# Sliding-window attention and a gated recurrence on one core: softmax division moved from the transposed layout to the values product's own layout

## The chip, the cores and the metric

The kernel runs on one core of a Trainium2 chip. The metric is device microseconds (us) of one execution, the median over runs. An engine is named as in the profile: PE is TensorE's matmul side and PEld its weight loads, DVE is VectorE, ACT is ScalarE, POOL is GpSimd, SP is SyncE, which here only issues DMAs.

## What is computed

Sixteen sequences of 512 tokens and 256 features pass through one block: attention with a window of 128 over 16 heads of 16 features, a residual and layernorm, a gated recurrence whose state runs from sequence to sequence, and a second residual and layernorm. Cut to the parts that matter here:

```python
# attention of one sequence; q, k, v: 16 heads x 512 x 16, blocks of 128 queries see 256 keys
scores = where(valid, q @ k.T / 4 + slope[h] * delta, -inf)
p = softmax(scores, axis=-1)          # exp(s - max) / sum
o = p @ v                             # 16 features per head
x1 = layernorm(x + o @ w_out.T)
# recurrence over the 16 sequences (t), state c: 512 x 256
f, i = sigmoid(x1 @ wf.T + c @ uf.T + bf), sigmoid(x1 @ wi.T + c @ ui.T + bi)
g = tanh(x1 @ wc.T + c @ uc.T + bc)
c = f * c + i * g
# after the last sequence
h = tanh(x1 @ wo.T + c_final @ uo.T + bo)
out = layernorm(x1 + h)
```

The division by the sum is not done on the probabilities. V carries a column of ones beside the 16 features of each head, so the product with the unnormalised probabilities gives, for each head, 16 context rows and one row of sums.

## The kernel before, in words

The program is written by hand for each engine, with semaphores; no scheduler reorders it. `iteration(t)` is written once per engine (lines from about 280, 380, 500, 745 and 1070) and all of them walk through 16 slots, `attend(0)` to `attend(15)`. A slot is one quarter of a group of four heads: on PE the raw scores of sequence t (L940), from which DVE takes the row maxima (L689), and, seven slots later, the scores with the maxima subtracted (L961), which ACT exponentiates (L448) and POOL cuts to the window (L347, L349). Between the slots stands the other work of several sequences: the qkv projections of t+1 and t, the values products and contexts of t-1, the output projection and layernorm of t-2, the gates (L921) and state update of t-3.

Four PSUM banks take everything that is not scores. They are used in two pairs, A0/A1 and B0/B1, which change names from iteration to iteration, so most waits on PE are waits for a bank to be emptied.

**The path of a context.** `values(t, g, bank)` (L975) makes, for group g of four heads, a bank of 128 rows: 32 rows per head, of which 16 are context, one the sum, the rest filler; the columns are the 512 queries. Because each head's sum is a row of that bank, and DVE works along rows, the kernel turns it: ACT copies the bank to `ctx_raw` (`ctx_out`, L459), PE transposes the four 128x128 blocks with the identity (`ctx_transpose`, L983), and DVE, with queries now on the partitions, takes reciprocals of the sum columns (L698) and multiplies (L703) into `o_tok`. This is `normalise`. Per sequence that is 16 transposes in four groups of four, which stand on PE after slots 0, 5, 8 and 13, each behind the values product of the next group. When all four groups are in `o_tok`, PE transposes it back (`o_transpose`, L1016, eight 128x128 blocks after slot 0) so that the features are on the partitions for the output projection, and ACT and DVE split it into a high and a low part (`ot_hi` L465, `ot_lo`, L661).

`ctx_raw` is a single buffer. `ctx_out` of a group waits until PE has transposed the group before it:

```python
wait(act, pv_ready, 4, t, g + 1)
wait(act, ct_ready, 4, t, g)
sc.activation(ctx_raw[:, :], bank[:, :], ACT.Copy).then_inc(ctx_done, 1)
```

On PE the gates of slot 1 write into bank A1, from which `ctx_out(t-1, 1)` reads, and so wait for it: `wait(pe, ctx_done, 4, t - 1, 2)`.

**The DMA queue.** SP issues nearly all DMAs in one order. Its busiest duty is to write q and k of each projection to DRAM (`parts_to_dram`, L239, two bursts of four DMAs of 256 KB per sequence) and read them back in the stacked layout that the scores need (`stack`, L254, four times eight DMAs). Each group's row maxima also go by DMA into the stack (`max_to_stack`, L262). SP is in order: what waits there holds everything written behind it.

After the 16 iterations `last_sequences` finishes the open sequences, and a last stage computes `h` and the second layernorm for all sequences. Wo and Uo, the weights of that stage, are loaded and split into high and low parts at the start.

## Time and profile before

| | |
|---|---|
| median of 3 runs | 1004.26 us (1003.01 to 1005.67) |
| the profiled execution, its own time | 1004.63 us |
| its span, first to last instruction | 1002.9 us |
| PE busy | 915.2 us, 91% |
| PEld busy | 753.2 us, 75% |
| DVE busy | 719.0 us, 72% |
| ACT busy | 575.9 us, 57% |
| POOL busy | 407.6 us, 41% |
| mean granted TensorE clock | 0.953 of full |
| moved by DMA | 131.86 MB |

The time of an execution is its span and 1.7 us around it. Busy shares are means over start, sixteen iterations, and end, each with its own limit; the iterations make up most of the span, and what limits one of them is read from its timeline.

### The profile page before, as it was taken

The page shows a single profiled execution, that of the slowest core. Times are in us where ns is not written, and L with a number is a line of the kernel's source. Part 1 is how long each engine was busy: PE and PEld are TensorE (multiplying, and loading weights), DVE is VectorE, ACT ScalarE, POOL GpSimd, SP SyncE. Part 2 cuts the span into 40 slices and gives each one's busy share as a digit, 9 for nine tenths or more (in the row PEclk, how much of TensorE's full clock was granted, in tenths as well). Part 3 has the DMA queues.
Part 4 walks back from the last instruction along what each step waited for, and adds up shares of the span by engine and source line. Part 5 has one row for each costly group of instructions (what it writes and reads, how often), then busy time and mean ns, then how long its engine had stood idle before and what let it go on. Part 6 is the DMA issues. An engine that isn't in the chain of part 4 may idle for free.

```text
span 1002.9 us, 25924 instructions
## 1 busy us (share of the span) xinstructions
PE 915.2 (91%) x9500; PEld 753.2 (75%) x9500; DVE 719.0 (72%) x2795; ACT 575.9 (57%) x1167; POOL 407.6 (41%) x687
## 2 busy tenths in 40 slices
PE   3587879999999999999999999999999989889994
PEld 2375668878788878788878787878787867668884
DVE  7766576877777777777777778787878673327885
ACT  5144556555656565656565656565756464325886
POOL 5142443354444444444444444444444353101443
PEclk9577889999999999999999999999999999899998
DMA  7634443535454545444544454444444400121764
GB/s 257 168 117 121 129 140 126 151 120 143 135 140 137 138 138 139 139 137 139 134 143 133 144 129 146 129 147 129 146 108 145 124 28 22 42 91 49 221 202 132
DMA packets 93534, 131.86 MB, mean 131 GB/s; under 512 B 12128, under 2 KB 47584, under 8 KB 93408
## 3 DMA queue, kind: packets, MB, share of 16 engines
q1 hardware_dynamic: 93136, 129.95, 44.2%
q8 instruction: 76, 1.25, 0.5%
q14 instruction: 50, 0.41, 0.1%
q10 hardware_dynamic: 272, 0.26, 0.1%
HBM read 79.31 MB, written 50.33 MB: 129 GB/s over the span
## 4 chain that ended last, share of the span: by engine, by line
PE 64%; DVE 25%; ACT 5%; issue 4%; POOL 2%; DMA 0%; ACTq 0%; DVEq 0%; POOLq 0%
PE bank L921 29%; DVE bank L689 11%; PE bank L909 11%; PE bank L940 8%; PE bank L975 7%; PE bank L961 3%; DVE max_q L689 3%; DVE qk_parts L661 2%; PE bank L983 2%; DVE gate L738 2%; DVE gate L736 1%; PE bank L1016 1%; PE bank L1029 1%; ACT Pt L643 1%; DVE stats L877 1%
## 5 line engine op out<-in xcount | busy, mean ns | idle before, releaser
L689 DVE CUSTOM_DVE_ANT_0 bank<-bank,mask 128x256 f32<-128x256 f32 (+1 forms) x1024 | 369.3, 423 | 136.1 <-PE bank L940 134.5
L448 ACT ACTIVATE Pt<-bank 128x512 f32<-128x512 f32 (+1 forms) x512 | 248.2, 536 | 204.1 <-PE bank L961 204.0
L347 POOL TENSOR_SCALAR_AFFINE_SELECT Pt<-Pt 128x512 f32<-128x512 f32 x256 | 174.7, 682 | 414.8 <-ACT Pt L448 414.8
L940 PE MATMUL bank<-Ks,Qs 59*128 59x256 f32 (+1 forms) x1024 | 149.5, 320 | 51.3 <-DVE max_q L689 40.5
L940 PEld LDWEIGHTS bank<-Ks,Qs 59*128 59x128 f32 x1024 | 108.5, 192 | 94.8 <-DVE max_q L689 54.5
L689 DVE DVE_READ_ACCUMULATOR2_ANT max_q<- 128x1 f32 x1024 | 144.6, 141 | 0.0
L349 POOL TENSOR_SCALAR_AFFINE_SELECT Pt<-Pt 128x384 f32<-128x384 f32 x256 | 139.3, 544 | 0.0
L975 PE MATMUL bank<-Pt,Vp 128*32 128x256 f32 (+1 forms) x2048 | 131.2, 377 | 0.0
L921 PE MATMUL bank<-x1T,Wg 64*128 64x512 f32 x960 | 128.0, 398 | 0.8 <-DVE o_tok L703 0.8
L921 PE MATMUL bank<-cT,Ug 64*128 64x512 f32 x960 | 125.8, 393 | 0.0
L961 PE MATMUL bank<-Qs,Ks 60*128 60x256 f32 (+1 forms) x1024 | 112.1, 271 | 0.4 <-ACT Pt L448 0.3
L975 PEld LDWEIGHTS bank<-Pt,Vp 128*32 128x32 f32 x2048 | 81.5, 116 | 32.1 <-issue 8.2
L921 PEld LDWEIGHTS bank<-cT,Ug 64*128 64x128 f32 x960 | 89.6, 184 | 17.7
L921 PEld LDWEIGHTS bank<-x1T,Wg 64*128 64x128 f32 x960 | 87.4, 185 | 18.6 <-DVE o_tok L703 0.9
L961 PEld LDWEIGHTS bank<-Qs,Ks 60*128 60x128 f32 x1024 | 95.7, 193 | 2.3 <-issue 1.3
L486 ACT ACTIVATE gate<-bank,bias_half 128x512 f32<-128x512 f32 x64 | 42.5, 687 | 44.7 <-PE bank L921 23.9
L459 ACT ACTIVATE ctx_raw<-bank 128x512 f32<-128x512 f32 x64 | 38.2, 597 | 49.7 <-PE bank L983 47.6
L909 PE MATMUL bank<-xT,Win 128*128 128x512 f32 x204 | 55.5, 425 | 8.6 <-DVE Win L661 8.6
L921 PE MATMUL bank<-Win,xT 64*128 64x256 f32 x768 | 56.7, 291 | 0.0
L909 PEld LDWEIGHTS bank<-xT,Win 128*128 128x128 f32 x204 | 40.5, 205 | 17.6 <-DVE Win L661 8.6
L921 PEld LDWEIGHTS bank<-Win,xT 64*128 64x128 f32 x768 | 52.8, 197 | 0.0
L661 DVE SCALAR_TENSOR_TENSOR qk_parts<-bank,qk_parts 128x512 fp32r<-128x512 f32 x64 | 42.6, 686 | 14.2 <-ACT qk_parts L431 14.2
(111 smaller groups left out, 1345.7 us busy)
## 6 DMA issues: line engine op xcount, KB each, us to landing
parts_dram<-qk_parts SPq DMA_DIRECT2D x128, 256.0 KB
Qs<-parts_dram SPq DMA_DIRECT2D x128, 128.0 KB, 2.6
Ks<-parts_dram SPq DMA_DIRECT2D x128, 128.0 KB, 2.7
xt_raw<-in_xt SPq DMA_DIRECT2D x16, 512.0 KB, 4.2
Qs<-parts_dram SPq DMA_DIRECT2D x128, 64.0 KB, 2.6
Ks<-parts_dram SPq DMA_DIRECT2D x128, 64.0 KB, 2.7
x_res<-in_x SPq DMA_DIRECT2D x16, 512.0 KB, 3.9
x_dram<-y SPq DMA_DIRECT2D x16, 512.0 KB, 3.7
```

What stands on the lines that cost most here:

```text
L347: gp.affine_select(out=p4[:, :, 0:128], in_=p4[:, :, 0:128], compare_op=ALU.is_ge, fill=0.0, base=0, pattern=[[0, 4], [1, 128]], channel_m ...
L349: gp.affine_select(out=p4[:, 0:3, 128:256], in_=p4[:, 0:3, 128:256], compare_op=ALU.is_ge, fill=0.0, base=0, pattern=[[0, 3], [-1, 128]], ...
L448: sc.activation(probabilities(g, 2 * pair + odd)[:, S * a:S * a + n], SC[odd][:, 0:n], ACT.Exp).then_inc(exp_done, 1)
L459: sc.activation(ctx_raw[:, :], bank[:, :], ACT.Copy).then_inc(ctx_done, 1)
L486: ins = sc.activation(gate[:, k if k == 3 else which, :], bank[:, :], ACT.Tanh, bias=bias_half[:, which, j:j + 1], scale=0.5)
L661: return ve.scalar_tensor_tensor(out_, in_, scale, hi.bitcast(F32), op0=ALU.mult, op1=ALU.subtract)
L689: ins = ve.tensor_tensor_reduce(out=raw, in0=raw, in1=mask[:, keys], scale=1.0, scalar=MASKED, op0=ALU.add, op1=ALU.max, accum_out=max_q[: ...
L909: ins = te.matmul(out_, w, m, start=(first and n == 0), stop=(last and n == len(todo) - 1))
L921: ins = te.matmul(out_, w(r), m(r), start=(turn == 0 and opens and n == 0), stop=final, skip_group_check=True)
L940: ins = te.matmul(MX[odd][:, 256 * (n % 2):256 * (n % 2) + 256][:, keys], Qs[rows, 2 * g + pair, n * WIN:(n + 1) * WIN], Ks[rows, 2 * g + ...
L961: ins = te.matmul(SC[odd][:, 256 * (j % 2):256 * (j % 2) + width], Ks[rows, 2 * g + pair, j * WIN:(j + 1) * WIN], Qs[rows, 2 * g + pair, j ...
L975: ins = te.matmul(bank[32 * hh:32 * hh + 32, j * WIN:j * WIN + width], Vp[:, j, PITCH * h:PITCH * h + 32], probabilities(g, hh)[:, 256 * j ...
```

## The change

The contexts stay in the layout in which the values product makes them. `ctx_transpose`, `o_transpose` and `normalise` go for sequences 0 to 14; for the last sequence they stay, under names that begin with `last_`. In their place:

- `store_ctx(t, g)`: SP writes `ctx_raw` to DRAM after each `ctx_out`; and `ctx_out` of a group now waits for the landing of the store of the group before it.
- `load_denominators`: SP waits for the four stores and gathers the 16 rows of sums, 512 queries each, as four blocks of 16 x 128 into `den_q`. DVE turns them (32x32 block transposes of a 128x128 tile), inverts them and turns them back; SP writes the result to DRAM (`store_inverses`) and, once that has landed, reads it back with each row repeated for the 16 features of its head (`spread_inverses`), twice 128x512.
- `load_contexts`: SP reads the context rows alone, packed, into `o_un`, twice 128x512.
- POOL multiplies the two (`scale_contexts`, twice 128x512, at the head of an iteration), and ACT and DVE split the product from SBUF into `oT` (`ot_hi` is moved behind slot 1, `ot_lo` behind slot 2).

Wo and Uo now share the place of Win and are loaded and split during the last sequences (ACT three activations, POOL two subtractions). The state update is cut in two: its first product (`forget`) is done earlier than the rest (`take_in`), after slots 0 and 6.

```diff
+            def store_ctx(t, g):
+
+                wait(sp, ctx_done, 4, t, g + 1)
+                sp.dma_start(ctx_dram[t % 2, g], ctx_raw[:, :]).then_inc(ctx_stored[g], 16)
+
+            def load_denominators(t):
+
+                sp.wait_ge(den_cleared, 1)
+                for g in range(QUADS):
+                    wait(sp, ctx_stored[g], 16, t, 16)
+                wait(sp, inv_stored, 16, t - 1, 16)
+                rows = ctx_dram[t % 2].rearrange("g (h r) (q i) -> q (g h) r i", r=2 * D, i=128)[:, :, D, :]
+                for q in range(4):
+                    sp.dma_start(den_q[32 * q:32 * q + H, :], rows[q]).then_inc(den_in, 16)
+
+            def load_contexts(t, c):
+                wait(sp, otlo_done, 2, t - 1, c + 1)
+                rows = ctx_dram[t % 2, 2 * c:2 * c + 2].rearrange("g (h r) s -> (g h) r s", r=2 * D)[:, 0:D, :]
+                sp.dma_start(o_un[:, c, :], rows).then_inc(o_un_in[c], 16)
+
+            def store_inverses(t):
+                wait(sp, inv_turned, 1, t, 1)
+                sp.dma_start(inv_dram[t % 2].rearrange("r (q i) -> q r i", i=128), den_q[:, :]).then_inc(inv_stored, 16)
+
+            def spread_inverses(t):
+
+                wait(sp, inv_stored, 16, t, 16)
+                for c in range(KC):
+                    wait(sp, scaled_done, 2, t - 1, c + 1)
+                    rows = inv_dram[t % 2, 8 * c:8 * c + 8]
+                    sp.dma_start(inv_den[:, c, :], rows.unsqueeze(1).to_broadcast([8, D, S])).then_inc(inv_in[c], 16)
+
...
                 p1, p2, n1, now = real(t - 1), real(t - 2), real(t + 1), real(t)
+                by_rows = p1 and t - 1 < B - 1
                 if p1: max_to_stack(t - 1, 3)
                 if now: stack(t, 1)
                 if p2:
                     wait(sp, y_done, 2, t - 3, 2)
                     sp.dma_start(x_res[:, :, :], x[t - 2].rearrange(tok, p=128)).then_inc(xres_in, 16)
+                if by_rows: store_ctx(t - 1, 1)
                 if real(t + 2): load_xt(t + 2)
                 if now:
                     stack(t, 2)
                     max_to_stack(t, 0)
-                    stack(t, 3)
+                if by_rows: store_ctx(t - 1, 2)
+                if now: stack(t, 3)
                 if n1: parts_to_dram(t + 1, 0)
                 if now: max_to_stack(t, 1)
+                if by_rows: store_ctx(t - 1, 3)
                 if p2:
                     wait(sp, x1_done, 4, t - 2, 4)
                     sp.dma_start(x1_dram[t - 2].rearrange(tok, p=128), y[:, :, :]).then_inc(x1_out, 16)
+                if by_rows:
+                    load_denominators(t - 1)
+                    for c in range(KC):
+                        load_contexts(t - 1, c)
                 if n1: stack(t + 1, 0)
                 if now: max_to_stack(t, 2)
-                if n1: parts_to_dram(t + 1, 1)
+                if by_rows:
+                    store_inverses(t - 1)
+                    spread_inverses(t - 1)
+                if n1:
+                    parts_to_dram(t + 1, 1)
+                    store_ctx(t, 0)
+                if t == B - 1: load_last_weights()
...
+            def scale_contexts(t, c):
+
+                wait(pool, o_un_in[c], 16, t, 16)
+                wait(pool, inv_in[c], 16, t, 16)
+                gp.tensor_tensor(o_un[:, c, :], o_un[:, c, :], inv_den[:, c, :], ALU.mult).then_inc(scaled_done, 1)
+
...
+                        scale_contexts(t - 2, c)
                 if p1:
                     for hh in range(4):
...
             def ctx_out(t, g, bank):
                 wait(act, pv_ready, 4, t, g + 1)
-                wait(act, ct_ready, 4, t, g)
+                pt, pg = before(t, g)
+                if pt < B - 1:
+                    wait(act, ctx_stored[pg], 16, pt, 16)
+                else:
+                    act.wait_ge(ct_ready, g)
                 sc.activation(ctx_raw[:, :], bank[:, :], ACT.Copy).then_inc(ctx_done, 1)
 
-            def ot_hi(t, c, bank):
+            def ot_hi(t, c):
                 if c == 0:
                     wait(act, op_ready, 2, t - 1, 2)
-                wait(act, ot_ready, 2, t, c + 1)
+                wait(act, scaled_done, 2, t, c + 1)
+                sc.activation(oT[:, 0, c, :], o_un[:, c, :], ACT.Copy).then_inc(othi_done, 1)
...
@@ -508,11 +607,11 @@
                 if p1: max_row(t - 1, 3, A0)
                 attend(0)
                 if p1: ctx_out(t - 1, 1, A1)
-                if p2:
-                    ot_hi(t - 2, 0, B0)
-                    ot_hi(t - 2, 1, B1)
                 attend(1)
                 if n1: x_hi(t + 1, 0)
+                if p2:
+                    ot_hi(t - 2, 0)
+                    ot_hi(t - 2, 1)
...
+            def turn_denominators(t):
+
+                wait(dve, den_in, 64, t, 64)
+                ve.transpose(den_t[:, :], den_q[:, :]).then_inc(den_turned, 1)
+
+            def invert_denominators(t):
+                wait(dve, den_turned, 1, t, 1)
+                own = den_t[:, :].rearrange("p (b r) -> p b r", r=32)[:, :, 0:H]
+                ve.reciprocal(own, own).then_inc(den_inverted, 1)
+
+            def turn_inverses(t):
+                wait(dve, den_inverted, 1, t, 1)
+                ve.transpose(den_q[:, :], den_t[:, :]).then_inc(inv_turned, 1)
+
+            def ot_lo(t, c):
+                wait(dve, othi_done, 2, t, c + 1)
+                minus_hi(oT[:, 1, c, :], o_un[:, c, :], oT[:, 0, c, :]).then_inc(otlo_done, 1)
+
...
+            def forget(t, j):
+
+                wait(dve, gate_done, 6, t, 3 * j + 1)
+                wait(dve, c_done, 2, t - 1, j + 1)
+                ve.scalar_tensor_tensor(gate[:, 3 * j, :], gate[:, 3 * j, :], 1.0, c2[:, j, :], op0=ALU.add, op1=ALU.mult).then_inc(kept_done, 1)
+
+            def take_in(t, j):
+                wait(dve, gate_done, 6, t, 3 * j + 3)
+                ve.scalar_tensor_tensor(gate[:, 1, :], gate[:, 1, :], 1.0, gate[:, 2, :], op0=ALU.add, op1=ALU.mult).then_inc(taken_done, 1)
+                wait(dve, kept_done, 2, t, j + 1)
+                wait(dve, taken_done, 2, t, j + 1)
+                wait(dve, chi_done, 2, t - 1, j + 1)
...
@@ -751,14 +878,14 @@
                     maxima(t, slot // 4, slot % 4)
 
                 attend(0)
-                if p1: normalise(t - 1, 0, A0)
-                if p2:
-                    ot_lo(t - 2, 0, B0)
-                    ot_lo(t - 2, 1, B1)
+                if p3: forget(t - 3, 0)
                 attend(1)
                 if n1: x_lo(t + 1, 0)
                 attend(2)
                 if n1: x_lo(t + 1, 1)
+                if p2:
+                    ot_lo(t - 2, 0)
...
                 attend(7)
-                if p3: update(t - 3, 0)
+                if p3: take_in(t - 3, 0)
                 attend(8)
-                if p3: update(t - 3, 1)
-                if p1: normalise(t - 1, 2, B0)
+                if p3: take_in(t - 3, 1)
                 attend(9)
                 attend(10)
                 attend(11)
                 attend(12)
                 if n1: qk_lo(t + 1, 2, B0)
                 attend(13)
+                if p1: turn_denominators(t - 1)
                 if n1: qk_lo(t + 1, 3, B1)
-                if p1: normalise(t - 1, 3, A0)
-                if p2:
-                    x1_lo(t - 2, 0, B0)
-                    x1_lo(t - 2, 1, B1)
+                if p1: invert_denominators(t - 1)
+                if p2: x1_lo(t - 2, 0, B0)
+                if p1: turn_inverses(t - 1)
+                if p2: x1_lo(t - 2, 1, B1)
...
-                    wait(pe, gate_done, 6, t - 3, 1)
-                    o_transpose(t - 2, 0, B0)
-                    freed(pe, (gate_done, 6, t - 3, 2), (ctx_done, 4, t - 1, 1))
-                    o_transpose(t - 2, 1, B1)
 
                 attend(1)
                 if p3:
                     g2, g3 = gate_halves(2, A0), gate_halves(3, A1)
-                    wait(pe, o_done, 4, t - 1, 1)
+                    wait(pe, maxrow_done, 4, t - 1, 4)
                     wait(pe, ctx_done, 4, t - 1, 2)
                     abreast(g2, g3, 0, None)
                 attend(2)
@@ -1094,19 +1214,19 @@
                 attend(3)
                 if p2:
                     o0, o1 = out_halves(0, B0), out_halves(1, B1)
+                    freed(pe, (gate_done, 6, t - 3, 1), (maxrow_done, 4, t - 1, 3))
+                    freed(pe, (gate_done, 6, t - 3, 2), (ctx_done, 4, t - 1, 1))
                     wait(pe, otlo_done, 2, t - 2, 2)
                     abreast(o0, o1, 0, None)
                 attend(4)
                 if p2: abreast(o0, o1, 1, op_ready)
 
                 attend(5)
-                freed(pe, (gate_done, 6, t - 3, 3), (o_done, 4, t - 1, 1), (qklo_done, 4, t, 3))
+                freed(pe, (gate_done, 6, t - 3, 3), (maxrow_done, 4, t - 1, 4), (qklo_done, 4, t, 3))
```

Two places of the order show what moves. The first is the end of an iteration on SP, before; `max_rows` are the row maxima of groups 2 and, behind the burst, 3, and `parts_dram` is where q and k go:

```order
L262 DMA Qs<-max_rows 1x8x128 [waits maxrow_done]
L262 DMA Qs<-max_rows 1x8x128
L239 DMA parts_dram<-qk_parts 8x16x512 [waits qklo_done,stacked3,stacked2]
L239 DMA parts_dram<-qk_parts 8x16x512
L239 DMA parts_dram<-qk_parts 8x16x512 [waits qklo_done]
L239 DMA parts_dram<-qk_parts 8x16x512
L262 DMA Qs<-max_rows 1x8x128 [waits maxrow_done]
L262 DMA Qs<-max_rows 1x8x128
L254 DMA Qs<-parts_dram 32x2x512 [waits q_parts_out0,sc_ready]
```

The same place after the change, where `ctx_raw` going to `ctx_dram` is `store_ctx(t, 0)`:

```order
L275 DMA Qs<-max_rows 1x8x128 [waits maxrow_done]
L275 DMA Qs<-max_rows 1x8x128
L300 DMA inv_dram<-den_q 4x32x128 [waits inv_turned]
L308 DMA inv_den<-inv_dram 128x1x512 [waits scaled_done,inv_stored]
L308 DMA inv_den<-inv_dram 128x1x512 [waits scaled_done]
L252 DMA parts_dram<-qk_parts 8x16x512 [waits qklo_done,stacked3,stacked2]
L252 DMA parts_dram<-qk_parts 8x16x512
L252 DMA parts_dram<-qk_parts 8x16x512 [waits qklo_done]
L252 DMA parts_dram<-qk_parts 8x16x512
L281 DMA ctx_dram<-ctx_raw 128x512 [waits ctx_done]
L275 DMA Qs<-max_rows 1x8x128 [waits maxrow_done]
L275 DMA Qs<-max_rows 1x8x128
```

Between the maxima of group 2 and the burst stand three DMAs with two waits, on DVE's second turn and on the landing of the inverses; the store of the context stands behind the burst and ahead of the maxima of group 3.

The second is PE from the end of slot 0's values product to the gates of slot 1, before:

```order
L975 MATMUL bank<-Pt,Vp 32x128 x4
L983 MATMUL bank<-ident,ctx_raw 128x128 [waits ctx_done,maxrow_done]
L983 MATMUL bank<-ident,ctx_raw 128x128 x3
L1016 MATMUL bank<-ident,o_tok 128x128 [waits o_done,gate_done]
L1016 MATMUL bank<-ident,o_tok 128x128 x3
L1016 MATMUL bank<-ident,o_tok 128x128 [waits o_done,gate_done]
L1016 MATMUL bank<-ident,o_tok 128x128 x3
L940 MATMUL bank<-Ks,Qs 128x256 [waits red_done] x2
L940 MATMUL bank<-Ks,Qs 128x256 x2
L961 MATMUL bank<-Qs,Ks 128x256 [waits exp_done] x2
L961 MATMUL bank<-Qs,Ks 128x256 x2
L921 MATMUL bank<-x1T,Wg 128x512 [waits ctx_done,o_done]
L921 MATMUL bank<-x1T,Wg 128x512 x11
```

and after:

```order
L1102 MATMUL bank<-Pt,Vp 32x256 [waits masked_done,x1lo_done]
L1102 MATMUL bank<-Pt,Vp 32x256 x11
L1102 MATMUL bank<-Pt,Vp 32x128 x4
L1067 MATMUL bank<-Ks,Qs 128x256 [waits red_done] x2
L1067 MATMUL bank<-Ks,Qs 128x256 x2
L1088 MATMUL bank<-Qs,Ks 128x256 [waits exp_done] x2
L1088 MATMUL bank<-Qs,Ks 128x256 x2
L1048 MATMUL bank<-x1T,Wg 128x512 [waits ctx_done,maxrow_done]
L1048 MATMUL bank<-x1T,Wg 128x512 x11
```

The twelve transposes are gone, and the gates, whose wait for `ctx_done` is the one for ACT's copy of group 1, come directly behind the scores of slot 1.

## Rows read from the trace of the kernel before

**Rows 1.** The page, busy time of each engine: us, share, instructions
```profile
PE 915.2 (91%) x9500; PEld 753.2 (75%) x9500; DVE 719.0 (72%) x2795; ACT 575.9 (57%) x1167; POOL 407.6 (41%) x687
```

**Rows 2.** Windows, 50 us of the middle: busy us (instructions) per engine, clock, DMA share
```profile
466.00:516.00 50.00, 48.97 (x571) 40.65 (x566) 38.65 (x162) 30.90 (x64) 22.22 (x38) 1.00 0.49 139
```

**Rows 3.** Timeline of PE, one iteration: start, us, what [idle before it]
```profile
480.17 1.66 PE L921 MATMUL bank<-x1T,Wg 64*128 64x512 f32 x12
...
492.93 0.66 PE L983 MATMUL bank<-ident,ctx_raw 128*128 128x128 f32 x4
493.34 3.02 PE L909 MATMUL bank<-xT,Win 128*128 128x512 f32 x12
...
505.29 0.66 PE L983 MATMUL bank<-ident,ctx_raw 128*128 128x128 f32 x4
505.87 0.51 PE L940 MATMUL bank<-Ks,Qs 59*128 59x256 f32 x4
...
508.54 0.32 PE L940 MATMUL bank<-Ks,Qs 59*128 59x128 f32 x1 [0.49 <-DVE max_q L689]
509.30 0.49 PE L940 MATMUL bank<-Ks,Qs 59*128 59x128 f32 x3 [0.44 <-DVE max_q L689]
...
518.28 1.35 PE L1029 MATMUL bank<-ident,y 128*128 128x128 f32 x8
...
528.53 0.66 PE L983 MATMUL bank<-ident,ctx_raw 128*128 128x128 f32 x4
...
529.99 0.51 PE L940 MATMUL bank<-Ks,Qs 59*128 59x256 f32 x4
...
530.64 1.67 PE L921 MATMUL bank<-x1T,Wg 64*128 64x512 f32 x12
```

**Rows 4.** Timeline of DVE, same iteration
```profile
518.23 0.69 DVE L661 SCALAR_TENSOR_TENSOR qk_parts<-bank,qk_parts 128x512 fp32r<-128x512 f32 x1
...
519.65 1.34 DVE L661 SCALAR_TENSOR_TENSOR x1T<-bank,x1T 128x512 fp32r<-128x512 f32 x2
```

**Rows 5.** Groups by line: busy us, mean ns of one, idle before
```profile
L364 POOL TENSOR_TENSOR cT<-c,cT 128x512 fp32r<-128x512 f32 x26 | 32.7, 1275 | 0.0
```

**Rows 6.** The page, DMA issues: KB each, median us to landing
```profile
Qs<-parts_dram SPq DMA_DIRECT2D x128, 64.0 KB, 2.6
...
x_dram<-y SPq DMA_DIRECT2D x16, 512.0 KB, 3.7
```

**Rows 7.** The tile parts_dram: landings min/median/max
```profile
DMA to landing us min/median/max: 2.0/2.7/5.1
```

**Rows 8.** Timeline of SP, same iteration: the time is that of issuing
```profile
483.75 0.43 SPq L275 DMA_DIRECT2D x_res<-in_x  x1
...
516.73 1.41 SPq L262 DMA_DIRECT2D Qs<-max_rows  x2
518.57 3.27 SPq L239 DMA_DIRECT2D parts_dram<-qk_parts  x4
```

**Rows 9.** Windows of 1 us behind that burst
```profile
521.00:522.00 1.00, 1.00 (x12) 0.78 (x12) 1.00 (x7) 0.15 (x1) 1.00 (x3) 1.00 0.51 190
525.00:526.00 1.00, 1.00 (x12) 0.79 (x10) 0.00 (x0) 0.00 (x0) 0.00 (x0) 1.00 0.52 199
526.00:527.00 1.00, 1.00 (x21) 0.88 (x21) 0.27 (x3) 0.55 (x1) 0.00 (x0) 1.00 0.19 68
```

**Rows 10.** Timeline of ACT, same iteration
```profile
529.28 0.60 ACT L459 ACTIVATE ctx_raw<-bank 128x512 f32<-128x512 f32 x1 [0.69 <-PE bank L983]
```

**Rows 11.** Windows near the end, behind a pause of PE
```profile
857.00:861.00 4.00, 3.75 (x28) 2.53 (x32) 1.38 (x2) 1.30 (x3) 0.00 (x0) 0.50 0.66 197
861.00:865.00 4.00, 4.00 (x36) 2.93 (x29) 0.00 (x0) 0.60 (x1) 0.00 (x0) 0.98 0.20 70
```

**Rows 12.** Timeline of PE near the end
```profile
857.25 1.94 PE L1029 MATMUL bank<-ident,y 128*128 128x128 f32 x8 [3.99 <-ACT y L470]
```

**Rows 13.** Timeline of DVE at the start
```profile
24.78 5.57 DVE L661 SCALAR_TENSOR_TENSOR cT<-c,cT 128x512 fp32r<-128x512 f32 x2 [1.16 <-ACT cT L613]
```

More of the change, by code:

```diff
@@ L299, in _ @@
             sp.wait_ge(xt_ready, 2 * B)
+            sp.wait_ge(last_lo, 2)
             def load(t, i):
@@ L606, in _ @@
                 qk_hi(0, k, banks[4 + (k + 2) % 4])
-            act.wait_ge(weights_in, 80)
-            for n in range(5):
+            act.wait_ge(weights_in, 48)
+            for n in range(3):
                 weights_hi(n)
```

172 lines of the change are left out of this document (96 added, 76 removed).

## The prediction

> **What bounds the kernel now.** I read the page first. PE is busy for 91% of the span [rows 1], and a stretch of 50 us in the middle, one iteration, says it more sharply: PE 48.97 of 50 us at full clock, DVE 38.65, ACT 30.90, POOL 22.22 [rows 2]. So in the iterations PE's own order of work sets the time, and everything else counts only where PE waits for it. The timeline of PE then shows what the change can take from it and where it waits: one iteration lasts 50.5 us (the gates of slot 1 begin at 480.17 and again at 530.64), and inside it PE waits only twice, 0.49 and 0.44 us, for DVE's maxima behind the state update and a `normalise` [rows 3]. All times below are on the clock of this iteration; sequence numbers are those of the code.
>
> **What goes.** Per iteration PE loses 16 context and 8 output transposes. I price them by start to next start, since they are pipelined: after slot 0, 528.53 to 529.99 = 1.46 us; after slot 5, 492.93 to 493.34 = 0.41; after slot 8, 505.29 to 505.87 = 0.58 [rows 3]. The fourth group, after slot 13, I price at nothing: the x1 transposes behind it need DVE's low part of k, which ends at 518.9, while the first of them starts at 518.28 [rows 3, 4]. Take the context transposes away, and PE arrives earlier and waits for DVE, which now also turns the sums there. The two waits of 0.93 us go too: `normalise` and the first product of the update are no longer in front of slot 9's maxima. Together 1.46 + 0.41 + 0.58 + 0.93 = 3.38 us per iteration. DVE and ACT lose and gain small instructions; with 11 and 19 us idle per iteration that costs nothing as long as they are not waited for. POOL gains two multiplications, 1.28 us each by its nearest row [rows 5], beside some 28 idle us; the windows behind them are of the group whose values product comes only after slot 5.
>
> **What is added, and what it waits for.** The price lies in one wait. `ctx_out(t, 1)` now needs the landing of `store_ctx(t, 0)`, and on SP that store stands at the very end of the iteration: behind `store_inverses`, behind its landing, behind two spreads and behind a burst of four stores of q and k. PE's gates of slot 1 wait for this `ctx_out`. I follow that chain.
>
> 1. DVE. The inverses are turned back behind the first low part of x1. The pair of those started at 519.65 and took 1.34 [rows 4], so the first ends at about 520.3. I take 520.4; SP has by then issued its row maxima (516.73 plus what is new ahead of it, about 1 us), so DVE comes last.
> 2. `store_inverses`, 64 KB, must land before SP goes on. No row shows this shape. The nearest is a 64 KB load of 2.6 us [rows 6]; it is cut into pieces of 2 KB, this one into four times as many of 512 B. The longest landing seen on this path is 5.1 [rows 7]. I take 3.3, near the first: 523.7.
> 3. Two spreads. An issue costs 0.43 us for a plain tile and 3.27 / 4 = 0.82 for the 8x16x512 pattern of the parts [rows 8]; these have that pattern on the DRAM side, so 1.6 together. The burst begins at 525.3 (at 0.43 each, 524.6).
> 4. The burst. The one issued from 518.57 keeps the DMA engines at a share of 0.51 to 0.52 and 190 to 199 GB/s from 521 on, and in the slice from 526 little is left (0.19) [rows 8, 9]. Its data end at 526.3, 7.7 us after the first issue: half the engines carry 1 MB, and issuing it faster would not help. The spreads' 512 KB have the same row count of 8; at 190 GB/s they take 2.75 us. The first data of a burst came 2.1 us after its issue, so theirs run from 525.8 to 528.5, and the burst's own first data (525.3 + 2.1 = 527.4) are pushed back by 1.15. End of the burst: 525.3 + 7.7 + 1.15 = 534.15.
> 5. `store_ctx(t, 0)`, 256 KB over all engines. Half of it lies on the engines that still carry the burst: 128 KB at 190 GB/s is 0.7, and 0.5 for the semaphore by my estimate: 535.35. If its share did not queue there, it would land 3.7 us at most after its own issue, the median of a store of 512 KB [rows 6]: 525.3 + 3.3 + 3.7 = 532.3.
> 6. ACT copies the bank, 0.60 [rows 10]: 535.95. PE's gates start at 536.0. Unforced they would have started at 530.64 - 1.46 = 529.2. PE waits 6.8 us.
>
> Step 5 is where a rule decides. The rows show only that half of the engines are busy while the parts go out, and with my reading that a later store waits for them the wait is 6.8. The Trainium skill says so too ("DMA: Bandwidth & Descriptors", HWDGE ordering): each engine consumes its descriptors in ring order. By that rule the store lands at 535.35 and the execution takes 1077; with a store that overtakes the burst the wait is 3.8 and the sum gives 1035. The same page (how many engines) makes the inverses' store, whose outer count is 4, run on 4 engines only; no row here shows such a store.
>
> **The clock.** When PE stood idle for 3.99 us near the end, the granted clock was 0.50 (1.2 GHz, of 2.4) for the 4 us after it went on, and 0.98 in the 4 us behind them [rows 11, 12]. Half the speed for 4 us costs 2.0. A wait of 6.8 us should do the same in each iteration.
>
> **The sum.** Per full iteration: - 3.38 + 6.8 + 2.0 = + 5.4; for t = 3 to 15, thirteen of them, + 70.5. Iteration 2 has the wait, but I count no clock loss, since its clock is unsteady already: + 3.4. Iteration 1 is bound by DVE, which loses four `normalise`: - 2. At the start DVE needed 5.57 us for two low parts of the state, whose like takes 0.68 later, beside POOL splitting the weights [rows 4, 13]; with Wo and Uo gone I take - 2. In the last sequences three activations come in front of the layernorm for which PE already waits [rows 12], 3 x 0.60 = + 1.8, the output transposes of sequence 14 go, - 1.0, and its contexts arrive late, + 1.5. Sum: 70.5 + 3.4 - 2 - 2 + 2.3 = + 72.2. The profiled execution took 1004.63 with a span of 1002.9; 1004.63 + 72.2 = 1076.8. The median of the runs is 0.4 below that execution, which changes nothing: **1077 us**.
>
> **Bounds.** With every step of the chain at its cheapest (2.6, two issues of 0.43, no push, but the burst in front: 523.0 + 0.86 + 7.7 + 0.7 + 0.5 = 532.75, gates at 533.4) PE waits 4.2 and an iteration costs + 2.8: 36.7 + 0.8 for iteration 2 - 1.7 for the rest is + 36, or 1040. With the dearest (a landing of 5.1, and two issues of 0.82) it waits 8.6: + 7.2, or 93.9 + 5.2 - 1.7 = + 97, 1102.
>
> **The rivals.**
> - *The store is in time, and the change is faster.* The place is the same: it decides whether `store_ctx(t, 0)` lands before 528.6, when the values product of the next group is done. Then 13 x 3.38 = 43.9, 3.4 in iteration 2 and 1.7 for the rest go: 956. For it speaks that PE is full and that what is taken away is PE's; against it, that even the cheapest chain with no queueing (523.0 + 0.86 + four issues of 0.82 + 3.7) gives 530.9. In between, with such a landing and a wait of 2.3 us, too short to cost much clock, an iteration still gains 1.1: 988. I give 0.08 to the first and 0.09 to the second.
> - *The wait is there, but short or without the clock.* The store does not queue, or PE's pause doesn't cost the clock: 6.8 without the clock is + 3.4 per iteration, 1051; 3.8 with the clock is + 2.4, 1035; 3.8 without it is + 0.4, 1009. What lies below 1040 has 0.15.
> - *The split of oT becomes the wait.* `ot_lo` now stands behind slot 2's maxima and is wanted in slot 3; if the store were in time, PE would wait there for some 0.5 us: 13 x 0.5 = 6.5 back, 962. It speaks for itself in the order, but behind a wait of 6.8 us in slot 1 it is hidden. It is in the chance of the first rival.
> - *DVE waits for the sums.* `turn_denominators` stands in DVE's row before slot 14. The fourth context lands at about 510, the gathers at 514, and DVE arrives at 518.4: 4 us to spare. Were it late, every us would be one of PE's: 0.04, above 1102.
>
> **How the numbers follow.** The main case, 1040 to 1102, has 0.64. A measurement of this kernel can tell 0.3%, 3 us, from no change. Slower by more: 0.64 + 0.04 + nearly all of the 0.15, so 0.81; same, 0.03; faster, 0.16. The range must leave out no more than 2 in 10: it takes in the main case and what lies below it down to 1005, where only the faster cases remain, and ends at 1102.
>
> **What would show it.** In the profile of the changed kernel, ACT's `ctx_raw` copy of group 1 should start about 7 us after the values product of slot 0 has ended, released by the DMA that stores group 0; PE's gates of slot 1 should show that idle time, and an iteration should last about 56 us with a granted clock near 0.95 and not 1.00. SP should wait for DVE's second turn and then for the landing of the inverses. The prediction is wrong if PE's longest wait per iteration is elsewhere, if the store lands less than 8 us after the first issue of the burst before it, or if the iterations are shorter than 50.5 us.

## The result and the profile after

The changed kernel takes **1137.06 us** (median of 4 runs, 1134.24 to 1141.48) against 1004.35 (1003.01 to 1005.67): a ratio of 1.1325, 95% interval 1.1286 to 1.1365. The forecast was 1077 and the range 1005 to 1102: the direction was right, the size missed by 60 us.

From the page of the changed kernel, busy time of the engines and the groups with the largest waits (columns as in [rows 5]):

```profile
PE 912.4 (80%) x9140; PEld 747.0 (66%) x9140; DVE 714.2 (63%) x2721; ACT 574.0 (50%) x1167; POOL 452.1 (40%) x717
...
L1048 PE MATMUL bank<-x1T,Wg 64*128 64x512 f32 x960 | 147.9, 445 | 91.1 <-ACT ctx_raw L543 91.1
...
L543 ACT ACTIVATE ctx_raw<-bank 128x512 f32<-128x512 f32 x64 | 37.9, 592 | 115.8 <-DMA ctx_dram<-ctx_raw 100.5
```

PE was busy for 91% [rows 1] and is now for 80%. The forecast wait is there: the gates wait 91.1 us for ACT's context copy, and the copy for the DMA. The waits of PE show what else there is (us in total, times, longest us):

```profile
PE bank L1048 <- ACT ctx_raw L543: 91.1, 14, 8.7
PE bank L1067 <- DVE max_q L789: 28.6, 52, 1.5
PE bank L1088 <- DMA Qs<-max_rows: 26.0, 19, 3.6
...
PE bank L1048 <- DVE oT L761: 14.1, 13, 2.0
```

L1088 is the second scores product, which waits for the row maxima on their way through SP's queue. No step of the forecast has that wait, and the one for oT was to be hidden. One iteration on SP shows the forecast chain. The first number of a row is the start of its first issue, the second the time that issuing took, and not the landing:

```profile
587.73 1.78 SPq L291 DMA_DIRECT2D den_q<-ctx_dram  x4
589.56 1.45 SPq L296 DMA_DIRECT2D o_un<-ctx_dram  x2
591.13 1.80 SPq L267 DMA_DIRECT2D Qs<-parts_dram  x4
592.97 1.82 SPq L267 DMA_DIRECT2D Ks<-parts_dram  x4
594.84 1.36 SPq L275 DMA_DIRECT2D Qs<-max_rows  x2
596.24 0.56 SPq L300 DMA_DIRECT2D inv_dram<-den_q  x1
601.24 1.27 SPq L308 DMA_DIRECT2D inv_den<-inv_dram  x2
602.62 4.01 SPq L252 DMA_DIRECT2D parts_dram<-qk_parts  x4
606.67 1.44 SPq L281 DMA_DIRECT2D ctx_dram<-ctx_raw  x1
608.16 2.74 SPq L275 DMA_DIRECT2D Qs<-max_rows  x2
```

and on PE, where the two waits stand 14 us apart; the last row is ACT's copy, which releases the second:

```profile
601.21 0.51 PE L1088 MATMUL bank<-Qs,Ks 60*128 60x256 f32 x4 [2.21 <-DMA Qs<-max_rows]
601.55 2.25 PE L1048 MATMUL bank<-cT,Ug 64*128 64x512 f32 x12
...
615.00 2.93 PE L1048 MATMUL bank<-x1T,Wg 64*128 64x512 f32 x12 [6.02 <-ACT ctx_raw L543]
```
```profile
614.25 0.60 ACT L543 ACTIVATE ctx_raw<-bank 128x512 f32<-128x512 f32 x1 [5.95 <-DMA ctx_dram<-ctx_raw]
```

The granted clock of the same stretch, in windows of 1 us (length, PE busy, clock, DMA share, GB/s); the windows left out in 604 and from 613 to 618 are all at 0.50:

```profile
601.00:602.00 1.00, 0.79 (x8) 1.00 0.00 0
602.00:603.00 1.00, 1.00 (x8) 0.59 0.15 55
603.00:604.00 1.00, 1.00 (x6) 0.50 0.46 174
...
605.00:606.00 1.00, 1.00 (x12) 0.71 0.48 152
606.00:607.00 1.00, 1.00 (x23) 1.00 0.49 176
...
612.00:613.00 1.00, 0.00 (x0) 0.71 0.78 256
...
618.00:619.00 1.00, 1.00 (x7) 0.50 1.09 402
619.00:620.00 1.00, 1.00 (x12) 0.88 0.27 94
620.00:621.00 1.00, 1.00 (x16) 1.00 0.00 0
```

About 1 us after PE has gone on behind the pause of 2.2 us, the clock falls to half (1.2 GHz) and stays there from about 602.2 to 605.6. PE, busy all the while, loses half of these 3.4 us, 1.7. In the pause of 6.0 us the clock falls at 612.4 and stays low until 619.2; 4.2 us of that are behind the pause, 2.1 us lost.

**An account of one iteration**, made the same way for every kernel below: from its PE timeline the period (x1 transposes to x1 transposes, mean of twelve iterations of the middle), the idle time before PE's instructions by releaser, and the rest. At full clock the rest is PE's own work, 46.4 to 46.5 us in the two kernels without the DMA path (x4, x8); what lies above that in the other kernels with the change is mostly the clock (the kernel before has its transposes there). Taken from the granted clock instead, as half of the time that PE was busy at half clock, the loss is 3.2 us an iteration in the changed kernel, 2.5 in x2, 0.7 in x11 and 0.1 in x7.

The columns between are waits: for ACT's context copy, for the row maxima, for Ks (the keys that `stack` reads back) and for oT (DVE's low part), each by the instruction that needs it; "x1 transposes" is what they wait for the low part of k, "DVE's maxima" what the raw scores wait for.

| kernel, us per iteration | period | wait for ctx_raw | row maxima | Ks | oT | x1 transposes | DVE's maxima | other | rest |
|---|---|---|---|---|---|---|---|---|---|
| before | 50.49 | 0 | 0 | 0 | 0 | 0 | 1.10 | 0.1 | 49.33 |
| changed | 60.38 | 7.00 | 1.66 | 0 | 0.93 | 0.71 | 0.60 | 0 | 49.48 |
| x1_early_store | 52.26 | 0.18 | 2.19 | 0.45 | 0.72 | 0.72 | 0.62 | 0 | 47.38 |
| x2_contexts_late | 58.68 | 7.70 | 0.23 | 0 | 0.92 | 0.69 | 0.62 | 0 | 48.51 |
| x3_both | 49.79 | 0.18 | 0.46 | 0.55 | 0.51 | 0.69 | 0.62 | 0 | 46.77 |
| x4_no_dma | 49.06 | 0.18 | 0.24 | 0 | 0.90 | 0.69 | 0.62 | 0 | 46.42 |
| x5_before_burst | 52.92 | 0.83 | 2.37 | 0 | 0.84 | 0.70 | 0.60 | 0 | 47.58 |
| x6_burst_first | 53.78 | 0.18 | 0.13 | 0 | 0 | 0.53 | 0.77 | 3.9 | 48.29 |
| x7_dve_order | 50.23 | 0.17 | 0.74 | 1.42 | 0 | 0.52 | 0.62 | 0 | 46.76 |
| x8_no_dma_order | 48.37 | 0.18 | 0.16 | 0 | 0 | 0.52 | 0.97 | 0 | 46.54 |
| x9_middle | 57.28 | 4.19 | 1.78 | 0 | 0.93 | 0.71 | 0.59 | 0 | 49.09 |
| x10_pool_queue | 53.64 | 0.18 | 0.23 | 0 | 0 | 0.52 | 0.82 | 3.2 | 48.70 |
| x11_sooner | 50.00 | 0.16 | 0.44 | 0.79 | 0 | 0.81 | 0.74 | 0 | 47.05 |

The "other" of x6 and x10 is a wait of the scores product for ACT's probabilities. Three numbers of the changed kernel's row (row maxima 1.66, oT and x1 transposes 1.64 together, and a rest 3.0 above 46.5) are the matter of the experiments.

### The profile page after: what moved, and what is told of

It reads as the page before. It is cut to its first block and busy times, and to the rows that moved or that the text cites. A ratio compares the mean times of both kernels' runs of the same rounds, so it can differ in the third digit from the quotient of the medians.

```text
span 1139.7 us, 25314 instructions
## 1 busy us (share of the span) xinstructions
PE 912.4 (80%) x9140; PEld 747.0 (66%) x9140; DVE 714.2 (63%) x2721; ACT 574.0 (50%) x1167; POOL 452.1 (40%) x717
## 5 line engine op out<-in xcount | busy, mean ns | idle before, releaser
L1048 PE MATMUL bank<-x1T,Wg 64*128 64x512 f32 x960 | 147.9, 445 | 91.1 <-ACT ctx_raw L543 91.1
L1067 PE MATMUL bank<-Ks,Qs 59*128 59x256 f32 (+1 forms) x1024 | 146.2, 323 | 44.9 <-DVE max_q L789 28.6
L1048 PEld LDWEIGHTS bank<-x1T,Wg 64*128 64x128 f32 x960 | 103.4, 213 | 110.8 <-issue 93.5
L415 POOL TENSOR_SCALAR_AFFINE_SELECT Pt<-Pt 128x384 f32<-128x384 f32 x256 | 146.2, 571 | 0.0
L1088 PE MATMUL bank<-Qs,Ks 60*128 60x256 f32 (+1 forms) x1024 | 114.5, 279 | 31.0 <-DMA Qs<-max_rows 26.0
L1048 PE MATMUL bank<-cT,Ug 64*128 64x512 f32 x960 | 139.2, 425 | 0.0
L1088 PEld LDWEIGHTS bank<-Qs,Ks 60*128 60x128 f32 x1024 | 95.6, 198 | 38.0 <-DMA Qs<-max_rows 30.2
L1048 PEld LDWEIGHTS bank<-cT,Ug 64*128 64x128 f32 x960 | 102.5, 206 | 18.5
L761 DVE SCALAR_TENSOR_TENSOR xT<-xt_raw,xT 128x512 fp32r<-128x512 f32 x32 | 23.3, 732 | 97.5 <-ACT xT L506 97.5
L436 POOL TENSOR_TENSOR o_un<-o_un,inv_den 128x512 f32<-128x512 f32 x30 | 39.0, 1301 | 96.7 <-DMA inv_den<-inv_dram 96.7
L1048 PE MATMUL bank<-Wout,oT 64*128 64x256 f32 x672 | 48.5, 287 | 14.1 <-DVE oT L761 14.1
```

The costliest lines, as they stand in the source:

```text
L415: gp.affine_select(out=p4[:, 0:3, 128:256], in_=p4[:, 0:3, 128:256], compare_op=ALU.is_ge, fill=0.0, base=0, pattern=[[0, 3], [-1, 128]], ...
L436: gp.tensor_tensor(o_un[:, c, :], o_un[:, c, :], inv_den[:, c, :], ALU.mult).then_inc(scaled_done, 1)
L1048: ins = te.matmul(out_, w(r), m(r), start=(turn == 0 and opens and n == 0), stop=final, skip_group_check=True)
L1067: ins = te.matmul(MX[odd][:, 256 * (n % 2):256 * (n % 2) + 256][:, keys], Qs[rows, 2 * g + pair, n * WIN:(n + 1) * WIN], Ks[rows, 2 * g + ...
L1088: ins = te.matmul(SC[odd][:, 256 * (j % 2):256 * (j % 2) + width], Ks[rows, 2 * g + pair, j * WIN:(j + 1) * WIN], Qs[rows, 2 * g + pair, j ...
```

## The experiments

Line numbers shift by one or two between the kernels; the operations are the same. SP's order of one iteration, as changed: the gather of the sums, the contexts' loads, `stack(t+1, 0)`, `max_to_stack(t, 2)`, the inverses' store, its landing, the spreads, the burst, `store_ctx(t, 0)`.

**x1_early_store** takes the store out from behind everything:

```diff
                 if now: max_to_stack(t, 2)
+                if n1: store_ctx(t, 0)
                 if by_rows:
                     store_inverses(t - 1)
...
                     parts_to_dram(t + 1, 1)
-                    store_ctx(t, 0)
```

> The change with store_ctx(t, 0) moved ahead of the inverses' store and the burst, directly behind the row maxima of group 2. Theory A (the place of this store on SP makes PE's wait in slot 1): the wait of PE's gates for ACT's ctx_raw copy, 7.0 us per iteration as a mean of twelve, goes with some 2.5 us of lost clock; the waits for the row maxima (about 2) and for oT (1.0) stay. An iteration falls from 60.4 to about 51, the kernel to about 1012 us. Theory B (the DMA engines are overloaded as a whole, wherever the store stands): the wait comes back at another landing, and the kernel stays above 1080.

Measured 1030.6 us (1024.71 to 1034.87), ratio 1.0257 (1.0217 to 1.0297), 19 us above the expected 1012. The wait for the context copy is gone, and 106 us with it, but the row maxima stayed and grew:

```profile
PE bank L1087 <- DMA Qs<-max_rows: 33.0, 21, 3.2
PE bank L1066 <- DVE max_q L788: 28.9, 53, 1.5
PE bank L1066 <- DMA Ks<-parts_dram: 21.9, 11, 11.5
PE bank L1047 <- DVE oT L760: 9.7, 10, 1.0
```

So the place of the store is the main cause, and not the only one.

**x2_contexts_late** asks where the maxima's wait comes from. The contexts' loads are the DMAs issued ahead of the stack and the maxima, and nobody needs them before the inverses:

```diff
                     load_denominators(t - 1)
-                    for c in range(KC):
-                        load_contexts(t - 1, c)
...
                     store_inverses(t - 1)
+                    for c in range(KC):
+                        load_contexts(t - 1, c)
                     spread_inverses(t - 1)
```

> The change with load_contexts (two loads of 256 KB with an outer count of 8) moved from ahead of the stack and the row maxima of group 2 to behind the inverses' store. If the maxima land late because these loads lie ahead of them on the engines, PE's wait for them (about 2 us in slot 15) goes. Theory A then says that the chain to the context's store still ends at the same distance from slot 13, so the wait in slot 1 grows by as much: 1125 to 1140. If the two waits are independent, some 35 us go: about 1100.

Measured 1113.68 us (1111.43 to 1117.89), ratio 1.1093. The maxima's wait fell from 1.66 to 0.23 us. And the landing of the inverses' store, for which SP stood still, fell too. SP's wait in the changed kernel, and here:

```profile
SPq L308 <- DMA inv_dram<-den_q: 55.6, 15, 4.8
```
```profile
SPq L308 <- DMA inv_dram<-den_q: 7.9, 15, 0.6
```

So it was not the store's shape: 512 KB of contexts' loads, with the stack behind them, had stood in its way. The spreads now start 2.5 us after the inverses' store, and not 5.0. Yet the context store gained nothing from it:

```profile
587.24 0.56 SPq L300 DMA_DIRECT2D inv_dram<-den_q  x1
587.84 1.25 SPq L296 DMA_DIRECT2D o_un<-ctx_dram  x2
589.71 1.19 SPq L308 DMA_DIRECT2D inv_den<-inv_dram  x2
591.01 2.47 SPq L252 DMA_DIRECT2D parts_dram<-qk_parts  x4
593.53 0.60 SPq L281 DMA_DIRECT2D ctx_dram<-ctx_raw  x1
```
```profile
602.76 0.60 ACT L543 ACTIVATE ctx_raw<-bank 128x512 f32<-128x512 f32 x1 [8.44 <-DMA ctx_dram<-ctx_raw]
```

The store is issued quickly, at 593.53, and it is 9.2 us from there to ACT's copy, which waits for its landing: the data of 2 MB issued in the 6 us before it are in front of it. So the wait did grow (7.00 to 7.70 us), by less than half of what the maxima gave back; with the second pause some clock loss went too (rest 49.48 to 48.51), and an iteration is 1.7 us shorter.

**x3_both** has both moves, with the context's store ahead of the inverses' store and the contexts' loads behind it.

> Both moves. Theory A: both waits go; an iteration is 47.1 (50.5 - 3.4) plus the 1.0 us wait for oT and perhaps 0.5 at the x1 transposes, 48.5 us: about 980 us, faster than before the change (1004). Theory B: above 1050.

Measured 998.33 us (996.93 to 1000.6), ratio 0.9947 (0.9929 to 0.9966): 139 us less than the changed kernel, and below the kernel before. With these two moves the change is a gain of half a per cent; 18 us of the expected gain are missing.

**x4_no_dma** says whether the DMA path keeps them. It drops `store_ctx` 1 to 3 and 0, the gathers, the loads, the inverses' store and the spreads, and fills `o_un`, `inv_den` and `den_q` with ones, so the attention output of sequences 0 to 14 is left out; POOL's, DVE's and ACT's instructions stay.

```diff
-                if by_rows: store_ctx(t - 1, 1)
...
-                wait(dve, den_in, 64, t, 64)
...
-                wait(pool, o_un_in[c], 16, t, 16)
-                wait(pool, inv_in[c], 16, t, 16)
+                wait(pool, otlo_done, 2, t - 1, c + 1)
```

> The change without its DMA path: no context, sum or inverse is stored or loaded for sequences 0 to 14, and ACT doesn't wait for a store; POOL multiplies tiles of ones, DVE turns and inverts a tile of ones, so that the attention output of these sequences is left out. It prices what the change takes off PE, with no new DMA. My sum gives - 3.38 us per iteration and 956 us. If it comes out near 1004, the transposes were worth nothing to begin with.

Measured 984.0 us (983.15 to 986.29), ratio 0.9801 (0.9784 to 0.9817). So even a free path would not give the forecast's 956. PE's work did shrink, by 49.33 - 46.42 = 2.9 us an iteration; but the waits behind it grew:

```profile
PE bank L1033 <- DVE oT L747: 13.8, 13, 2.0
PE bank L1141 <- DVE qk_parts L747: 8.9, 13, 0.8
```

**x5_before_burst** splits the chain of the context store. It puts the store behind the inverses' landing and the spreads, as changed, but ahead of the burst.

```diff
                 if n1:
-                    parts_to_dram(t + 1, 1)
                     store_ctx(t, 0)
+                    parts_to_dram(t + 1, 1)
```

> The only edit to the changed kernel: store_ctx(t, 0) moves from behind the burst of four stores of q and k to directly ahead of it, still behind the store of the inverses, its landing and the two spreads. Theory A (the burst in front of it on the queue and on half the DMA engines is what delays the store; the inverses' chain alone would do no harm): the store is issued near the place where the first store of the burst stood, lands some 4 us later, before the values product of slot 0 has ended, and PE's wait for the context copy (7.0 us an iteration) goes, with its clock loss: 1030 to 1040 us, as with the store ahead of the whole chain (1030.6). Rival B (the landing of the inverses and the spreads' 512 KB are enough by themselves to make it late): a wait of 2 to 4 us stays with its clock loss of some 2 us, 1070 to 1095 us.

Measured 1035.56 us (1029.48 to 1039.06), ratio 1.0307 (1.0272 to 1.0342): theory A. The inverses' landing still costs SP 56.7 us, and PE hardly waits for ctx_raw (0.83).

**x9_middle** puts the store between the two stores of q and the two of k.

```diff
                 for which in range(2):
+                    if which and between is not None: store_ctx(between, 0)
...
-                    parts_to_dram(t + 1, 1)
-                    store_ctx(t, 0)
+                    parts_to_dram(t + 1, 1, t)
```

> The only edit to the changed kernel: store_ctx(t, 0) goes into the middle of the burst, behind its two stores of q and ahead of its two of k. Behind the whole burst PE waited 7.0 us an iteration for it (1137.1 us), ahead of the burst hardly at all (1035.6). Theory A (the store's data queue behind whatever was issued before it): half a burst in front is 512 KB on half of the engines, 3.9 us of data less than a whole one, so PE waits some 3 us an iteration and the time is 1080 to 1095 us, clock loss included. Rival B (only the time of its own issue counts, 2 us earlier than behind the burst, and the data don't queue): a wait of 5 us stays, 1105 to 1120 us.

Measured 1101.59 us (1096.58 to 1103.11), ratio 1.0965: between the two theories, with a wait of 4.2 where they had 3 and 5. From the start of the store's issue to ACT's copy in one iteration of each, when ACT stood waiting for it: 5.2 us with only the spreads in front (599.95 to 605.17 in x5), 6.6 with half a burst (586.17 to 592.72), 7.6 with a whole one (606.67 to 614.25), and 9.2 in x2. The median landing of all context stores in x3 is 3.5. So both act: the store leaves SP later, and its data are held up by what is in front. The Trainium skill ("DMA: Bandwidth & Descriptors", HWDGE ordering) says that each DMA engine consumes its descriptors in ring order, and this growth is in accord with it; a store that overtook what is in front would have kept one landing time in all of them. That the transfers in flight merely share the engines' time would lengthen the landing too, and these runs don't tell the two apart.

**x7_dve_order** is x3 with two moves on DVE.

```diff
-                if n1: x_lo(t + 1, 1)
                 if p2:
                     ot_lo(t - 2, 0)
                     ot_lo(t - 2, 1)
+                if n1: x_lo(t + 1, 1)
...
-                if p1: turn_denominators(t - 1)
                 if n1: qk_lo(t + 1, 3, B1)
+                if p1: turn_denominators(t - 1)
```

> The kernel with both moves on SP's queue (998.3 us), and two moves on DVE: ot_lo(0) and ot_lo(1) ahead of x_lo(t + 1, 1) instead of behind it, and turn_denominators behind qk_lo(t + 1, 3) instead of ahead of it. Theory: PE's wait of 0.4 to 1.0 us for oT in slot 3 and some 0.25 of the 0.75 us before the x1 transposes go, so about 0.9 us in each of 13 iterations: 986 us. Rival: what PE saves there it spends waiting for the row maxima and for Ks of the stack, since the DMA's times don't move: 995 to 998 us.

Measured 1002.55 us (996.75 to 1006.32, 12 runs), ratio 0.9982 (0.9963 to 1.0001): the rival, and 4.6 us above its range. The wait for oT went (0.51 to 0), and Ks and the row maxima took it over (1.01 to 2.16 together).

**x8_no_dma_order** makes the same two moves where no DMA can take over (x4).

> The kernel without the DMA path of the contexts (984.0 us; tiles of ones stand in for the loaded contexts and inverses, so the attention output of sequences 0 to 14 is left out), with the same two moves on DVE as in x7_dve_order. It asks why that kernel gained 20 us and not the forecast 48. Theory A: 1.0 us an iteration is the wait for oT and 0.3 us the turn of the sums ahead of the low part of k, 13 x 1.3 = 17 us: 967 us. Rival B: PE's order has other dependences on DVE and ACT that take over, and it stays at 980 to 984 us.

Measured 975.79 us (973.39 to 977.05), ratio 0.9715 (0.9697 to 0.9734). The 0.9 for oT went; of the wait at the x1 transposes only 0.17, since they then wait for the low part of k itself, and DVE's maxima took 0.35. With the clock full and no DMA in the way, 2.8 us less work for PE (49.33 - 46.54) shortened the iteration by 2.1.

**x6_burst_first** and **x10_pool_queue** try to start the burst sooner, on x7. The first moves it ahead of the inverses' store and the contexts' loads:

```diff
+                if n1: parts_to_dram(t + 1, 1)
                 if by_rows:
                     store_inverses(t - 1)
...
                     spread_inverses(t - 1)
-                if n1: parts_to_dram(t + 1, 1)
```

> The kernel of x7_dve_order with one more move on SP: the burst parts_to_dram(t + 1, 1) goes ahead of the inverses' store, the contexts' loads and the spreads. Theory A: the burst starts some 3 us earlier, so Ks and the row maxima behind it land earlier and PE's waits for them (0.4 to 1.1 us each) go; the spreads land late, but before ot_lo is wanted: 975 to 982 us. Rival B: the inverses' chain behind a burst of 1 MB lands 6 us or more later, oT is late for slot 3, and PE waits there 2 to 4 us with a clock loss: 1010 to 1050 us.

> The kernel of x7_dve_order with the inverses' store and the two spreads issued by POOL instead of SP (store ahead of the last four windows of the iteration, spreads behind them), so that SP doesn't wait for their landing and the burst is issued some 4 us earlier. Theory A: Ks and the row maxima behind the burst land earlier, their waits (some 2 us an iteration) go, and the inverses, on a queue of their own, are not held up: 975 to 985 us. Rival B: the DMA engines are shared all the same, the inverses and spreads land late behind the burst's data, oT is late and PE waits at slot 2 or 3, as with the burst first (1055 us): 1010 us or more.

x6 measured 1055.08 us (1047.41 to 1062.31), x10 1041.65 (1038.02 to 1047.05), ratios 1.0507 (1.0472 to 1.0543) and 1.0371 (1.0349 to 1.0392): rival B both times, x6 even 5 us above its range. Ks is in time, but the inverses and the spreads are behind the burst. In x10, whose inverses have a queue of their own, POOL's rows of one iteration read:

```profile
602.40 1.22 POOL L427 DMA_DIRECT2D inv_den<-inv_dram  x2 [0.40 <-DMA inv_dram<-den_q]
610.58 1.29 POOL L433 TENSOR_TENSOR o_un<-o_un,inv_den 128x512 f32<-128x512 f32 x1 [6.96 <-DMA inv_den<-inv_dram]
613.47 1.26 POOL L433 TENSOR_TENSOR o_un<-o_un,inv_den 128x512 f32<-128x512 f32 x1 [1.60 <-DMA inv_den<-inv_dram]
```

8.2 us from the spreads' issue to the first product, where x3 has 6.05 (569.98 to 576.03). ACT waits for the products at `ot_hi`, and with it, in order, the probabilities that PE wants: 3.9 and 3.2 us an iteration. So a queue of their own did not help: the spreads still landed late behind the burst's data, which SP had issued from 598.20 on. That the shared DMA engines hold them up is the reading that fits; no run separates it from another cause on POOL's queue.

**x11_sooner** leaves the order of the queue and starts the inverses earlier, on x7:

```diff
                 attend(12)
+                if p1:
+                    turn_denominators(t - 1)
+                    invert_denominators(t - 1)
+                    turn_inverses(t - 1)
                 if n1: qk_lo(t + 1, 2, B0)
...
-                if p1: turn_denominators(t - 1)
-                if p1: invert_denominators(t - 1)
...
-                if p1: turn_inverses(t - 1)
...
+                if by_rows: store_inverses(t - 1)
                 if now: max_to_stack(t, 2)
                 if n1: store_ctx(t, 0)
                 if by_rows:
-                    store_inverses(t - 1)
```

> The kernel of x7_dve_order with the sums turned, inverted and turned back in a row directly behind slot 12's maxima, in DVE's gap of 0.9 us before qk_lo(t + 1, 2), some 3 us sooner than now, and the inverses' store ahead of max_to_stack(t, 2) on SP. Theory A (PE's remaining waits for Ks and the row maxima, 2.2 us an iteration, come from the burst starting late behind the spreads): the inverses are stored 2 us sooner, the spreads and the burst start 1 to 1.5 us sooner, and 1 to 1.5 us of those waits go: 983 to 990 us. Rival B: the fourth gather of the sums lands only about when DVE gets there, DVE waits for it, and PE waits for the low part of k and the x1 transposes in turn: 1000 to 1015 us.

Measured 995.9 us (990.57 to 1000.38), ratio 0.9922 (0.9893 to 0.9952): short of theory A, and 0.8% below the kernel before. Its median is the lowest of the complete versions here, but its interval overlaps that of x3 (0.9929 to 0.9966), so the two are not told apart. Against x7, Ks and the row maxima together fell from 2.16 to 1.23 us an iteration, while the x1 transposes (+ 0.29), DVE's maxima (+ 0.12) and the rest (+ 0.29) gave most of that back. The rest is the clock: in the twelve iterations of x11 it was at half five times, from 333.7, 364.4, 408.8, 756.9 and 808.1, for 3.4 us each, the first four behind pauses of PE of 1.4 to 2.1 us. In x7 that happened once.

## Why the prediction was right and wrong

**The wait in slot 1** was forecast in its place and size: 6.8 us against 7.0. The size is right by luck. In the iteration shown, from the inverses' issue (step 1) to ACT's copy (step 6), the forecast has 535.35 - 520.4 = 14.95 us, the trace 614.25 - 596.24 = 18.0:

- step 2, the landing of `store_inverses`: 3.3 forecast, 5.0 measured. The step failed by taking the price from the size of the transfer and not from what is issued ahead of it. With the contexts' loads out of the way the spreads start 2.5 us behind it (x2).
- step 3, two spreads: 1.6, measured 1.38.
- steps 4 and 5, burst and store: 10.05, measured 11.63 (602.62 to 614.25). Right in kind (x5, x9); the issues alone grew to 4.01 + 1.44, from 3.27 [rows 8] and 0.43.

The chain was 3.05 us longer, but PE reached the place 3.9 later as well, by the 2.2 us of its other wait and 1.7 of clock: 6.8 + 3.05 - 3.9 = 5.95, and the row shows 6.02.

**The sum per iteration** was + 5.4; it is + 9.9 (60.38 - 50.49). The step that failed is the one that let a single wait carry the price: the row maxima's way through the same queue was counted as nothing once SP had issued them, and it costs 1.66 us of waiting and 0.7 to 1.0 us of clock an iteration. Term by term against the account:

| term | forecast | measured |
|---|---|---|
| transposes gone | - 2.45 | - 2.9 (49.33 - 46.42, x4) |
| DVE's waits gone | - 0.93 | - 0.57 (with o_tok) |
| wait for ctx_raw | + 6.8 | + 7.0 |
| wait for the row maxima | not in the sum | + 1.66 |
| oT, "hidden" | 0 | + 0.93 |
| x1 transposes | 0 | + 0.71 |
| clock | + 2.0 | + 3.0 |

1. *Missing: the row maxima.* This is the largest flaw of the working. "SP has by then issued its row maxima" was said of the issue alone. They are issued at 594.84 and PE goes on at 601.21, 6.4 us later, because they stand behind contexts' loads and a stack. x2 shows it by 1.43 us of wait less with one move.
2. *oT.* "Behind a wait of 6.8 us in slot 1 it is hidden" is wrong: the wait passes through ACT, and `ot_hi` stands behind `ctx_out` there, so oT is late by as much as PE is. 0.93 us stay with the wait of slot 1 and 0.90 without it (x4); the move on DVE takes them away (x7, x8). The forecast had 0.5.
3. *Slot 13 "at nothing"* holds as a net price: PE's work fell by 0.4 more than the three other groups make, and 0.71 of waiting came for it.
4. *The clock.* 2.0 us for one long pause is what a kernel with one such pause shows: x2, rest 48.51 against 46.5. The changed kernel has 3.0. In five of the twelve iterations the clock is at half for another 3.4 us behind a wait of 1.9 to 2.4 us for the row maxima, 1.7 us lost each time, or 0.7 an iteration of the 1.0. So the term was about right for the long pause, and there was one too few, which goes back to point 1. The rivals took "a wait of 2.3 us" to be "too short to cost much clock"; here one of 2.2 us cost 1.7.

The differences are - 0.4 + 0.4 + 0.2 + 1.7 + 0.9 + 0.7 + 1.0 = 4.5 us an iteration, or 58 us for 13. The span grew by 136.8 us (1139.7 - 1002.9), 64.6 more than the forecast 72.2; the profiled execution is the longest of the four. Of the 6.6 that remain, the start has most: up to the x1 transposes of iteration 2 the forecast had - 0.6 us, which is what the kernel without the DMA path shows (x4, 162.2 against 162.9), but with it they come at 171.9, + 9.0. There PE waits already, 3.55 us for row maxima at 121.53 and 4.31 us for ACT's probabilities at 134.73, which stand behind a context copy that had waited 7.71 us for its store. The first of the thirteen iterations grew by only 7.2 (59.5 against 52.4), and the end by 2.1, as forecast.

**The rivals.** "The store is in time" was x3: 998, not the 956 to 962 forecast. The range's lower part rested on a gain of 3.38 us an iteration; x4 shows 1.4 and x8, with two better places on DVE, 2.1. What failed is the reading that what leaves a full PE leaves the iteration: behind each piece of it DVE, ACT or a DMA was late by up to 1 us as soon as PE came earlier.

Open is why the rest of x3 and x7, with hardly any half clock, lies 0.3 us above that of x4 and x8, and how much of a store's 5.2 to 9.2 us is queueing on the DMA engines and how much is SP's own hand-over; a store on another queue in the same place was not tried.

## What to carry to other kernels

On a DMA queue that issues in order, price a transfer by what was issued just before it, not by its own size; so go through every transfer behind the place where new ones are put in, the tiny ones too, and ask who waits for its landing. Put what the critical engine waits for ahead of new traffic that nobody needs soon: here two such moves took back 139 us, more than the 133 that the change had cost. And where an engine is full, work taken off it is worth only as much as its neighbours' slack: try it with the replacement free of cost before building the replacement.

## What the runs showed of the hardware

- Behind a pause of PE of 2.2 us the granted clock was at half for 3.4 us, 1.7 us lost; the low clock of the pause of 6.0 us cost 2.1 (windows above). A pause of that kind doesn't always cost it: behind one of 3.0 us in x1 the clock stayed full, and in x11 it fell behind one of 1.4 us. What decides between them is open.

```profile
381.96 0.50 PE L1087 MATMUL bank<-Qs,Ks 60*128 60x256 f32 x4 [3.01 <-DMA Qs<-max_rows]
```
```profile
382.00:384.00 2.00, 2.00 (x20) 1.00 0.05 9
384.00:386.00 2.00, 2.00 (x29) 1.00 0.51 168
```
- Issuing a DMA takes longer behind a burst: the same context store 0.43 us at 583.92 and 1.44 at 606.67; the two maxima 1.36 us at 594.84, 2.74 at 608.16.

```profile
583.92 0.43 SPq L281 DMA_DIRECT2D ctx_dram<-ctx_raw  x1
```

- The 64 KB store in four blocks of 32x128 lands within about 2.4 us with little in front of it (x2: issued at 587.24, the spreads issued at 589.71; x3: at 567.50 and 569.98).
- On DVE the turn of a 128x128 tile takes 0.30 us and the reciprocal of 128x64 0.53; low parts of oT, whose source is now in SBUF, take 1.03 us each in the mean (0.69 to 1.12), and those of the last stage, from PSUM, 0.68.
